# PSUM as the scratch of the small normalisation chains in step 0 of a layer-norm, convolution and attention kernel

## The reference, cut to what matters

```python
def _L0_conv_ref(x, gn_gamma, gn_beta, qkv_w, qkv_b, proj_w, proj_b):
    xf = x.reshape(b, c, t)
    qkv = conv1d_same(group_norm(xf, gn_gamma, gn_beta), qkv_w, qkv_b)   # 16 taps, 768 outputs
    h = qkv_attention(qkv.reshape(b * NUM_HEADS, -1, t)).reshape(b, -1, t)
    return (xf + conv1d_same(h, proj_w, proj_b)).reshape(b, c, *spatial) # 5 taps
...
x = x + _L0_conv_ref(_ln_c(x), ...)     # _ln_c: normalise over channels, eps 1e-6
t = _to_tokens(x)
t = t + _L0_ffn_ref(_ln_t(t))           # a lookup on a few columns of each token
x = _from_tokens(t, x)
```

## Time and profile before

| | |
|---|---|
| median of 3 runs | 1068.02 us (1067.68 to 1069.91) |
| the profiled execution | 1067.8 us |
| its span, first to last instruction | 1066.0 us |
| mean granted TensorE clock | 0.961 |
| busy over the span: PE, DVE, ACT, POOL | 935.6, 745.2, 666.5, 340.1 us |
| busy in the first 170 us: PE, DVE, ACT, POOL | 110.48, 141.29, 98.68, 90.55 us |

### The profile page before, as it was taken

One profiled execution on the slowest core, in us unless ns is written; L12 is line 12 of the kernel. 1 busy time (PEld: TensorE's weight loads), 2 busy tenths in 40 slices (PEclk: granted clock), 3 DMA queues, 4 the chain that ended last, 5 costly groups with the idle time before them and its releaser, 6 DMA issues.

```text
span 1066.0 us, 19610 instructions
## 1 busy us (share of the span) xinstructions
PE 935.6 (88%) x7826; PEld 744.5 (70%) x7826; DVE 745.2 (70%) x1230; ACT 666.5 (63%) x1112; POOL 340.1 (32%) x225
## 2 busy tenths in 40 slices
PE   2586679988999779999998999999999989999864
PEld 1475567756877557777776778877788768777653
DVE  6999876654674467878777565566557566778877
ACT  5756366566566547867787666576657666576631
POOL 2766642331352025526550121110112105323320
PEclk9989799989999989999999999999999999999987
DMA  7040133756677754747544754735465862452412
GB/s 282 29 181 22 60 114 98 182 135 182 155 198 167 180 157 104 155 116 211 144 105 79 181 128 94 154 93 110 98 162 109 228 164 59 111 129 68 112 60 80
DMA packets 291866, 138.32 MB, mean 130 GB/s; under 512 B 269120, under 2 KB 271552, under 8 KB 291264
## 3 DMA queue, kind: packets, MB, share of 16 engines
q1 hardware_dynamic: 291776, 137.08, 51.0%
HBM read 48.80 MB, written 16.95 MB: 62 GB/s over the span
## 4 chain that ended last, share of the span: by engine, by line
PE 36%; DVE 32%; ACT 15%; issue 8%; DMA 5%; SPq 2%; POOL 1%; ACTq 0%; DVEq 0%; POOLq 0%
PE cM L1233 9%; PE cQ L1233 8%; PE cP L1233 8%; DVE W L1513 5%; ACT arena L1109 5%; DVE smx L1708 4%; DMA wsum<-w_qkv 4%; DVE arena L1685 4%; PE psS L1370 3%; PE psT L1370 3%; PE psV L1347 2%; SPq L535 2%; ACT arena L914 2%; PE psV L1351 2%; DVE arena L1559 1%
## 5 line engine op out<-in xcount | busy, mean ns | idle before, releaser
L1233 PE MATMUL cM<-U,W 128*128 128x256 f16 x1728 | 207.6, 278 | 30.7 <-DVE U L1521 18.1
L1233 PEld LDWEIGHTS cM<-U,W 128*128 128x128 f16 x1728 | 171.1, 99 | 65.6 <-DVE U L1521 18.4
L1233 PE MATMUL cQ<-U,W 128*128 128x256 f16 x1728 | 207.8, 277 | 8.9 <-DVE W L1513 6.2
L1233 PE MATMUL cP<-U,W 128*128 128x256 f16 x1728 | 204.2, 276 | 8.7 <-DVE W L1513 4.9
L1233 PEld LDWEIGHTS cQ<-U,W 128*128 128x128 f16 x1728 | 170.2, 99 | 42.9 <-DVE W L1513 6.8
L1233 PEld LDWEIGHTS cP<-U,W 128*128 128x128 f16 x1728 | 169.5, 98 | 41.4 <-ACT y_all L969 4.9
L1685 DVE SCALAR_TENSOR_TENSOR arena<-arena,smx 128x1024 f16<-128x1024 f32 x128 | 174.8, 1366 | 14.8 <-ACT arena L1119 14.4
L724 POOL TENSOR_TENSOR ap<-ap 128x512 f32<-128x512 f32 x24 | 39.7, 1655 | 397.7 <-ACT ap L981 397.5
L1119 ACT ACTIVATE arena<-arena,smx 128x1024 f16<-128x1024 f32 x128 | 147.0, 1148 | 4.3
L1708 DVE TENSOR_REDUCE smx<-psS 128x1 f32<-128x1024 f32 x64 | 78.0, 1218 | 60.1 <-PE psS L1370 59.7
L1102 ACT ACTIVATE smx<-smx,tiny 128x1 f32<-128x1 f32 x128 | 37.3, 291 | 125.3 <-DVE smx L1708 124.9
(11 more groups left out here) (215 smaller groups left out, 1329.9 us busy)
## 6 DMA issues: line engine op xcount, KB each, us to landing
U<-kept_u SPq DMA_DIRECT2D x21, 520.0 KB, 5.7
staging<-w_qkv SPq DMA_DIRECT2D x20, 512.0 KB, 5.7
wsum<-w_qkv SPq DMA_DIRECT2D x24, 256.0 KB, 4.1
U<-kept_u SPq DMA_DIRECT2D x7, 780.0 KB, 5.0
kept_u<-temp_b SPq DMA_DIRECT2D x9, 520.0 KB, 3.5
arena<-x_tok SPq DMA_DIRECT2D x8, 512.0 KB, 6.8
arena<-arena SPq DMA_DIRECT2D x16, 256.0 KB, 3.6
W<-x_tok SPq DMA_DIRECT2D x4, 1024.0 KB, 5.7
```

What stands on the lines that cost most here:

```text
L1233: last = mm(out, W[:, j, wl, c, QTAPS * (3 * family + third) + tap, :], u[:, ul, c, at + tap:at + tap + QUART], start=((g, c, t) in OPENER ...
```

## The change

The numbers of the chains in step 0 move from SBUF to two unused pieces of the PSUM tile `psV`: `early` (three rows of ten) and `early_a`, `early_b`. Each operation in them that had two SBUF tensors as inputs now has at least one in PSUM, or is written as a `tensor_scalar` whose second number comes in as a per-partition scalar. In the layer norm one operation is added (a `tensor_copy` of rstd back to `ln` in SBUF, as ScalarE reads it from there), and ScalarE waits for two increments of `z_nm` in place of one. In the group norm two pairs of `tensor_tensor` become pairs of one-element `tensor_scalar`, and of the `group_stats` pair the second no longer waits for the first; `group_mean` waits for two increments. ScalarE's eight square roots read and write PSUM. `w_add` and the last operation of `w_scale` become `tensor_scalar`. The last stage, outside step 0, stays in SBUF.

```diff
+        early = psV[:, 3 * P:3 * P + 30].rearrange("p (r k) -> p r k", r=3)
+        early_a, early_b = (psV[:, 3 * P + 32 + CT * q:3 * P + 32 + CT * (q + 1)] for q in range(2))
...
-            nc.vector.tensor_scalar(nt[:, 0, at:at + var.shape[-1]], var, eps, None, ALU.add).then_inc(S[asked], 1)
+            nc.vector.tensor_scalar(work[:, 0, :], var, sign, eps, ALU.mult, ALU.add).then_inc(S[asked], 1)
...
-            n, s, q = (nt[:, r, at:at + out.shape[-1]] for r in range(3))
+            n, s = (work[:, r, :] for r in range(2))
             eng.wait_ge(S[sq_done], runs)
             ch.step(v.reciprocal(q, s))
             ch.step(v.tensor_tensor(s, n, q, ALU.mult))
...
-                a(nt[:, 1, at:at + width], nt[:, 0, at:at + width], ACT.Sqrt).then_inc(S[done], 1)
+                a(work[:, 1, :], work[:, 0, :], ACT.Sqrt).then_inc(S[done], 1)
...
-                act.wait_ge(S["z_nm"], q + 1)
+                act.wait_ge(S["z_nm"], 2 * (q + 1))
...
-                rstd_end(ch, dve, ln[:, b, :, 1], 0, "ln_sq", q + 1)
+                rstd_end(ch, dve, early[:, 2, 0:8], early[:, :, 0:8], nt[:, 2, 0:8], "ln_sq", q + 1)
                 ch.end()
-                v.scalar_tensor_tensor(nmr[:, b, :], ln[:, b, :, 0], -1.0, ln[:, b, :, 1], ALU.mult, ALU.mult) \
+                v.tensor_copy(ln[:, b, :, 1], early[:, 2, 0:8]).then_inc(S["z_nm"], 1)
+                v.scalar_tensor_tensor(nmr[:, b, :], ln[:, b, :, 0], -1.0, early[:, 2, 0:8], ALU.mult, ALU.mult) \
...
-                ch.step(v.tensor_tensor(gs[:, :, 2], gs[:, :, 0], gs[:, :, 0], ALU.mult))
-                v.tensor_tensor(gs[:, :, 1], gs[:, :, 1], gs[:, :, 2], ALU.add).then_inc(S["gstat_done"], 1)
+                for c in range(CT):
+                    v.tensor_scalar(gs[:, c, 1:2], gs[:, c, 0:1], gs[:, c, 0:1], gs[:, c, 1:2], ALU.mult, ALU.add) \
+                        .then_inc(S["gstat_done"], 1)
...
-                ch.step(v.tensor_tensor(gn[:, :, 2], gn[:, :, 0], gn[:, :, 0], ALU.mult))
-                ch.step(v.tensor_tensor(gn[:, :, 3], gn[:, :, 1], gn[:, :, 2], ALU.subtract))
-                rstd_ask(gn[:, :, 3], 1e-5, 8, "gn_var")
+                for c in range(CT):
+                    ch.done(v.tensor_scalar(gn[:, c, 3:4], gn[:, c, 0:1], gn[:, c, 0:1], gn[:, c, 1:2], ALU.mult, ALU.subtract))
+                ch.wait()
+                rstd_ask(gn[:, :, 3], 1e-5, early[:, :, 8:10], "gn_var", -1.0)
...
-                rstd_end(ch, dve, gn[:, :, 1], 8, "gn_sq", b + 1)
-                ch.step(v.tensor_tensor(gn[:, :, 1], gn[:, :, 1], par[:, 0, :], ALU.mult))
-                ch.step(v.tensor_tensor(gn[:, :, 2], gn[:, :, 0], gn[:, :, 1], ALU.mult))
-                ch.step(v.tensor_tensor(gn[:, :, 2], par[:, 1, :], gn[:, :, 2], ALU.subtract))
+                rstd_end(ch, dve, early[:, 2, 8:10], early[:, :, 8:10], nt[:, 2, 8:10], "gn_sq", b + 1)
+                ch.step(v.tensor_tensor(early_a, early[:, 2, 8:10], par[:, 0, :], ALU.mult))
+                ch.step(v.tensor_tensor(early_b, gn[:, :, 0], early_a, ALU.mult))
+                ch.step(v.tensor_tensor(early_b, par[:, 1, :], early_b, ALU.subtract))
...
-                    v.tensor_tensor(am[:, 0:1], am[:, 4:5], am[:, 5:6], ALU.add).then_inc(S["wam_done"], 1)
+                    v.tensor_scalar(am[:, 0:1], am[:, 4:5], am[:, 5:6], None, ALU.add).then_inc(S["wam_done"], 1)
...
-                v.tensor_tensor(isc[:, m:m + 1], wsc[:, 1, m:m + 1], usc[:, 1:2], ALU.mult) \
+                v.tensor_scalar(isc[:, m:m + 1], wsc[:, 1, m:m + 1], usc[:, 1:2], None, ALU.mult) \
```

More of the change, by code:

```diff
@@ L248, in pow2, with rstd_ask, rstd_end @@
             ch.step(v.tensor_scalar(inverse.bitcast(I32), bits[:, 0:1], 1.0, -k * EXP23, ALU.mult, ALU.add))
-        def rstd_ask(var, eps, at, asked):
-            nc.vector.tensor_scalar(nt[:, 0, at:at + var.shape[-1]], var, eps, None, ALU.add).then_inc(S[asked], 1)
-        def rstd_end(ch, eng, out, at, sq_done, runs):
+        def rstd_ask(var, eps, work, asked, sign=1.0):
+            nc.vector.tensor_scalar(work[:, 0, :], var, sign, eps, ALU.mult, ALU.add).then_inc(S[asked], 1)
+        def rstd_end(ch, eng, out, work, q, sq_done, runs):
             v = nc.vector
-            n, s, q = (nt[:, r, at:at + out.shape[-1]] for r in range(3))
+            n, s = (work[:, r, :] for r in range(2))
             eng.wait_ge(S[sq_done], runs)
@@ L834, in _, with sqrt @@
             a = nc.scalar.activation
-            def sqrt(asked, done, runs, width, at=0):
+            def sqrt(asked, done, runs, work):
                 act.wait_ge(S[asked], runs)
-                a(nt[:, 1, at:at + width], nt[:, 0, at:at + width], ACT.Sqrt).then_inc(S[done], 1)
+                a(work[:, 1, :], work[:, 0, :], ACT.Sqrt).then_inc(S[done], 1)
             def ln_root(q):
-                sqrt("ln_var", "ln_sq", q + 1, 8)
+                sqrt("ln_var", "ln_sq", q + 1, early[:, :, 0:8])
             def gn_root(q):
-                sqrt("gn_var", "gn_sq", q + 1, CT, 8)
+                sqrt("gn_var", "gn_sq", q + 1, early[:, :, 8:10])
             def normal(q):
                 b = BATCH_AT[q]
-                act.wait_ge(S["z_nm"], q + 1)
+                act.wait_ge(S["z_nm"], 2 * (q + 1))
                 for i in range(8):
@@ L931, in last_stage @@
                 if kind == "norm":
-                    sqrt("f_var", "f_sq", b + 1, RUNS[b][2])
+                    sqrt("f_var", "f_sq", b + 1, nt[:, :, 0:RUNS[b][2]])
                 if kind == "ob":
@@ L1161, in group_mean @@
             def group_mean(b):
-                pe.wait_ge(S["gstat_done"], b + 1)
+                pe.wait_ge(S["gstat_done"], CT * (b + 1))
                 if b:
@@ L1415, in layer_norm @@
                 ch.wait()
-                rstd_ask(ln[:, b, :, 1], 1e-6, 0, "ln_var")
+                rstd_ask(ln[:, b, :, 1], 1e-6, early[:, :, 0:8], "ln_var")
             def layer_norm_end(q):
                 ch, b = norm_chains[q], BATCH_AT[q]
-                rstd_end(ch, dve, ln[:, b, :, 1], 0, "ln_sq", q + 1)
+                rstd_end(ch, dve, early[:, 2, 0:8], early[:, :, 0:8], nt[:, 2, 0:8], "ln_sq", q + 1)
                 ch.end()
-                v.scalar_tensor_tensor(nmr[:, b, :], ln[:, b, :, 0], -1.0, ln[:, b, :, 1], ALU.mult, ALU.mult) \
+                v.tensor_copy(ln[:, b, :, 1], early[:, 2, 0:8]).then_inc(S["z_nm"], 1)
+                v.scalar_tensor_tensor(nmr[:, b, :], ln[:, b, :, 0], -1.0, early[:, 2, 0:8], ALU.mult, ALU.mult) \
                     .then_inc(S["z_nm"], 1)
-            group_chains = [Chain(dve, "c_g", b, 19) for b in range(NB)]
+            group_chains = [Chain(dve, "c_g", b, 18) for b in range(NB)]
             def group_stats(b):
@@ L1445, in group_norm @@
                                       psV[:, 0:2 * CT].rearrange("p (k c) -> p k c", k=2)))
[L1446 to L1448 removed]
+                for c in range(CT):
+                    ch.done(v.tensor_scalar(gn[:, c, 3:4], gn[:, c, 0:1], gn[:, c, 0:1], gn[:, c, 1:2], ALU.mult, ALU.subtract))
+                ch.wait()
+                rstd_ask(gn[:, :, 3], 1e-5, early[:, :, 8:10], "gn_var", -1.0)
             def group_norm_end(b):
                 ch = group_chains[b]
[L1452 to L1455 removed]
+                rstd_end(ch, dve, early[:, 2, 8:10], early[:, :, 8:10], nt[:, 2, 8:10], "gn_sq", b + 1)
+                ch.step(v.tensor_tensor(early_a, early[:, 2, 8:10], par[:, 0, :], ALU.mult))
+                ch.step(v.tensor_tensor(early_b, gn[:, :, 0], early_a, ALU.mult))
+                ch.step(v.tensor_tensor(early_b, par[:, 1, :], early_b, ALU.subtract))
                 wait(dve, "eo_done", 4 * b)
[L1457 to L1458 removed]
+                ch.done(v.tensor_scalar(ab[:, :, 0], early_a, usc[:, 0:1], None, ALU.mult))
+                v.tensor_scalar(ab[:, :, 1], early_b, usc[:, 0:1], None, ALU.mult).then_inc(S["ab_done"], 1)
                 ch.end()
@@ L1617, in last_stage @@
                 if kind == "norm":
-                    rstd_ask(stats[:, :, 1], 1e-5, 0, "f_var")
-                    rstd_end(ch, dve, stats[:, :, 1], 0, "f_sq", run + 1)
+                    rstd_ask(stats[:, :, 1], 1e-5, nt[:, :, 0:count], "f_var")
+                    rstd_end(ch, dve, stats[:, :, 1], nt[:, :, 0:count], nt[:, 2, 0:count], "f_sq", run + 1)
                     ch.step(v.scalar_tensor_tensor(nmr[:, b, i0:i0 + count], stats[:, :, 0], -1.0, stats[:, :, 1], ALU.mult,
```

## The result

The changed kernel takes 1051.89 us (median of 4, 1051.18 to 1053.36) where the kernel before takes 1067.85 us in the same comparison. The medians lie 15.96 us apart. The ratio is 0.985 with a 95% interval of 0.983 to 0.987, which is 16.2 us less, between 14.4 and 18.0. The profiled execution took 1052.32 us, its span 1050.5 against 1066.0.

The account below looks back on a forecast made before the run. VectorE, standing for GpSimd's operations, was taken to set step 0's pace until 136 us. Gains of 15.0 less 0.4 us for copies gave 14.6 us off 1067.8; median forecast 1053.4 us, own range 1050.5 to 1057, wider range 1050 to 1061.

Parts of the forecast that it names:

- third layer norm: Step 0: request's 0.84 us wait only changes places, two waits at its end (1.85 us) fall to about 0.2; gained 1.6 us.
- `w_add`: At 76.84 us in step 0: waits 1.07 us with weight splits behind it, so nothing gained.
- second group norm: Step 0: four waiting operations freed, batch statistics behind them don't wait for GpSimd; all 3.9 us gained.
- fourth layer norm: Step 0: waits of 1.9 + 1.8 and 0.9 us go, the split then waits about 1 us; gained 3.5 us.
- third group norm: Step 0: waits of 2.0 us and 4.3 us go, splits wait 1.0 us more; gained 5.3 us.
- fourth group norm: Step 0: 1.7 us waited, but a split and the key split behind wait about as long instead; gained 0.
- What came back: Of 20.9 us of waits in step 0, 5.9 us return in later operations needing GpSimd's to be over, mostly weight splits.
- The price of PSUM: 76 small VectorE operations now touching `psV` cost 0 extra; far end 0.06 us each, 4.6 us.
- That the waits come back in full: Rival: six chains' following two-SBUF-input operations wait 1.7 us each, 10.2 us together; 1060.1 us, chance 0.14.
- Slow PSUM: Rival: small operations in PSUM cost 0.06 us more for each of 76; 1058.0 us, chance 0.12.
- the slower case: Rival: PSUM writes followed by a wait for their own end, at 0.3 us each, give 1076.2 us; chance 0.03.
- That the lock stays: Rival: an operation with one PSUM tensor waits for GpSimd as with two SBUF ones; 1068.4 us, chance 0.06.

Follow-up runs that it names:

- the second execution: The changed kernel, unedited, run and profiled again on another chip: 1049.85 us, ratio 0.985 to the kernel before.
- scales alone: Kernel before with only `w_add` and the last operation of `w_scale` as `tensor_scalar`: 1066.47 us, ratio 1.000, step 1 earlier by 0.04 us.
- the two kernels without waits: Kernel before and changed kernel, each with GpSimd's step 0 `tensor_tensor` cut to two elements per dimension: 1031.71 and 1031.57 us.
- the group norms alone: Kernel before with only the four group norms' chains changed: 1058.47 us, ratio 0.992, step 1 earlier by 9.35 us.
- the last experiment: Changed kernel with the last operation of `w_scale` put back to a `tensor_tensor` with two SBUF inputs: 1051.64 us, ratio 0.986.
- the layer norms alone: Kernel before with only the four layer norms' chains in PSUM: 1060.66 us, ratio 0.995, step 1 earlier by 5.70 us.

## Why the prediction was right, and where its terms were off

The mechanism and the sum stood: 16.1 us off step 0 where 14.6 were forecast, and some 15 of them are the change's own. Taking the differences of the same instruction's start, before and after, from chain to chain gives each term. That the sum came so close is in part luck: `w_add` lost 1.2 us where nothing was forecast, and four of the other terms came out 0.5 to 0.7 us too small.

| term | forecast us | measured us | from |
|---|---|---|---|
| second layer norm | 0.7 | 0.4 | split behind it 42.59, now 42.17 |
| third layer norm | 1.6 | 2.1 | group statistics 70.07, now 67.52 |
| `w_add` | 0 | -1.2 | reciprocal 85.85, now 84.46 |
| second group norm | 3.9 | 3.9 | `L1410` 91.62, now 86.32 |
| fourth layer norm | 3.5 | 4.2 | group statistics 104.19, now 94.65 |
| third group norm | 5.3 | 6.0 | next statistics 126.04, now 110.46 |
| fourth group norm | 0 | 0.5 | split behind it 135.44, now 119.34 |
| copies into `ln` | -0.4 | in the terms above | `L1424` to `L1425` 0.08 us |
| sum, before rounding | 14.6 | 16.1 | |

- **The second group norm** was exact, because what lies behind it, `L1410`, never waits for the lock.
- **The third layer norm** hid a gain that I had dropped. I wrote that the last operation of `w_scale` "once loses a wait of as much: I leave it out". It is 0.21 us and was 0.28, and that moved the split at 52 us ahead of GpSimd, 1.28 us in place of 2.26. What failed here is to price an operation by its length alone where the next one competes for a lock. The runs show that it didn't matter in the end: scales alone 0.04 us, and 0.1 us when taken out of the changed kernel.
- **`w_add`** failed. I counted what GpSimd would do and not what SyncE would: the loads start 3.3 us earlier and collide with the store, and VectorE waits 2.94 us for them (2.35 in the second execution). I had warned that transfers move with step 0's end, but not looked at the queue in its middle. The price is 1.2 us by the next chain, since the splits behind took 1.41 us where they had taken 2.50. This is also why the second group norm ended 5.3 us earlier and not the 6 that were to show. Taking the wait away brought no time that could be measured.
- **The fourth layer norm and the last two group norms** gave 0.7, 0.7 and 0.5 us more than forecast, all in the same direction. In the fourth layer norm the split waits 0.7 us where I had about 1. In the third group norm 2.1 us of idle time on VectorE behind the chain went too (below), about 1 us of it TensorE's clock, against splits that wait some 1.6 us more. Without that 1 us the term is 5.0 where 5.3 was forecast. In the fourth 1.7 us of waits went, and 0.8 + 0.1 came back: 0.75 us became 1.56 in the split at 113.67, and the key split at 116.02 takes 1.41 us where 1.28 is free.
- **What came back** was to show as about 6 us more in the splits' sum. It is 2.5 us. The account closes in another way: of 20.9 us of waits, 2.5 came back in splits of the weights, some 0.6 in the two operations at 108.71 and 116.02, 2.9 as idle time at `w_add` and 0.4 are the copies, while idle time of 1.25 + 1.33 us before two operations at 123.43 and 126.04 fell to 0.51: 20.9 - 2.5 - 0.6 - 2.9 - 0.4 + 2.1 = 16.6, against 16.1 measured, which leaves 0.5 us open. (Added up anew, the fifteen groups hold 21.0 us and not 20.9, which changes none of this.) I had counted 5.9 + 0.4 = 6.3 us to go this way, and 6.4 did. That is luck, as 2.9 of them lie at `w_add`, where I had none. What I hadn't counted at all are the 2.1 us of idle time that went as well, half of which belongs to the clock in one execution.

VectorE before those two, in the kernel before:

```profile
123.43 1.28 DVE L1556 SCALAR_TENSOR_TENSOR arena<-y_all,tiny,arena 64x1024 f16<-64x1024 f32 x1 [1.25 <-ACT arena L914]
126.04 1.30 DVE L1432 BATCH_NORM_STATS2 st<-psS 128x6 f32<-128x512 f32 x2 [1.33 <-PE psT L1157]
```

and in the changed one:

```profile
108.71 1.71 DVE L1561 SCALAR_TENSOR_TENSOR arena<-y_all,tiny,arena 64x1024 f16<-64x1024 f32 x1 [0.51 <-ACT arena L916]
110.46 1.30 DVE L1435 BATCH_NORM_STATS2 st<-psS 128x6 f32<-128x512 f32 x2
```

- **The price of PSUM** was taken as 0 and its far end as 4.6 us. It is at most 7 ns an operation, which makes no more than 76 x 7 ns = 0.5 us. In the Trainium skill the page "VectorE: DVE Perf Modes", section on the TRN2 errata, would have made it 62 cycles, an estimated 65 ns each; the 174 against 168 ns of the two kernels without waits don't agree, and the measurement decides. (Its figure is for operations that read PSUM, which 68 of the 76 do; the other 8 only write it.)
- **The rivals.** That the waits come back in full (1060.1) falls: not 7.9 but 16 us were gained. Slow PSUM (1058.0) falls by the 174 ns, and so does the slower case. That the lock stays falls by the same row. A gain above 17 us, which had 0.03, came nearer than any of them.
- **TensorE's clock** was to get no worse, as TensorE is idle less in step 0. It doesn't show: from 26 us to step 1's start the granted clock is 0.90 before, and 0.89 and 0.96 in the two executions after. Between those two step 1 starts at 143.02 and 143.09, so the difference doesn't show in step 0's length. It does where VectorE waits for TensorE, as before the last group statistics of the kernel before.
- **The others keep up**: of the earlier trace rows, ScalarE no longer waits 3.78 us for `ab`, and TensorE waits 1.43 us in place of 5.32:

```profile
90.11 0.33 PE L1159 MATMUL psS<-ident_sb,arena 128*128 128x128 f32 x1 [1.43 <-ACT arena L867]
```

## What to carry to other kernels

Where small operations on VectorE run beside long ones on GpSimd, look at their mean time by form: a few numbers per partition that take 0.9 us are waiting, and scratch in PSUM, or a `TENSOR_SCALAR` over one element with per-partition scalars, frees them: they took 0.17 to 0.27 us here. Count of the freed waits only what isn't needed again by the next operation with two inputs in SBUF, and go on along the chain to the next statistics or other work that doesn't need GpSimd's operation to be over: about three quarters of the time were kept here. Then ask which buffers come free earlier and what their loads will run into.

## What the runs showed that I had not expected

**One tenth of a microsecond decides a turn, and the turn is not kept.** In two kernels the split at 52 us, some 0.1 us earlier or later at the lock, took 1.28 us or 2.26, and both times the microsecond was gone further down.

**ScalarE is quicker in PSUM.** The square root of eight numbers takes 167 ns on average from PSUM to PSUM in the changed kernel; from SBUF to SBUF it took 210 in the kernel before. One of them in the changed kernel:

```profile
56.86 0.16 ACT L840 ACTIVATE psV<-psV 128x8 f32<-128x8 f32 x1 [1.78 <-DVE psV L254]
```

**The clock at step 1's start differs between executions of one kernel.** The granted clock in the 4 us from the first matmul on, in the changed kernel's first profile (columns as at the top):

```profile
143.02:147.02 4.00, 4.00 (x24) 3.02 (x25) 1.20 (x3) 3.34 (x5) 0.00 (x0) 0.62 0.88 357
```

and in its second, on another chip:

```profile
143.09:147.09 4.00, 4.00 (x37) 3.55 (x38) 0.71 (x2) 2.86 (x5) 0.00 (x0) 1.00 0.79 320
```

At 0.62, between the two levels of 1.2 and 2.4 GHz, 24 matmuls fit where 37 do at 1.00, and the first 36 take 5.76 us in place of 4.11: 1.65 us with the same instructions. TensorE had been idle for 2.20 us in the first and for 2.69 in the second, so the longer stall doesn't go with the lower clock. The kernel before (0.57), the group norms alone (0.62) and the last experiment (0.62) have it low as well, the others at 1.00. It is not all of the spread behind step 0: the layer norms alone have 1.00 at this point and still 906.9 us behind it, where the second execution of the changed kernel has 904.4. Which executions fall which way wasn't settled. A difference of under 2 us between two medians of this kernel should not be put down to an edit before the profiles have been compared up to step 1's start and behind it.
